# Row of s2 spread by two transfers through DRAM, reciprocals spread by SBUF transfers, no negated means, new places of the steps

## What is computed

```python
# layer 0: additive attention           x: (32, 256, 128), adj: (32, 256, 256) int
Wh = h @ W.T;  s1 = Wh @ a1;  s2 = Wh @ a2
e = leaky_relu(s1[:, :, None] + s2[:, None, :], 0.2);  e = where(adj == 0, -inf, e)
x = layernorm(x + softmax(e) @ Wh)
# layer 1: bilinear attention logits, softmax, two products, ELU
x = layernorm(x + elu(x @ W_1 + (att @ x) @ W_2))
# layer 2: attention with 4 heads of 32, output projection, ReLU
out = concat_heads(softmax(mask(q @ k.T * scale)) @ v)
x = layernorm(x + relu(out @ Wo + bo))
# layer 3: relational convolution; with relation 1 alone it is
v = (h + b) * sigmoid(g + bg);  x = layernorm(x + relu((adj == 1).T @ v))
```

## Time and profile before

| what | value |
|---|---|
| median of three runs | 498.07 us (496.0 to 498.63) |
| the profiled execution | 496.9 us, span of its instructions 495.0 us |
| PE, ACT, DVE, POOL busy | 95%, 86%, 83%, 75% |
| mean granted TensorE clock | 0.988 of full speed |
| mean DMA rate | 54 GB/s |

### The profile page before, as it was taken

The page is one execution under the profiler, slowest core; times in us unless marked ns, Lnnn a source line. Parts: engine busy times, 40 slices in busy tenths (PEclk is TensorE's granted clock), DMA queues, the critical chain, the costliest instruction groups (busy, mean ns, idle before and its releaser), DMA issues. The chain is left out here.

```text
span 495.0 us, 13988 instructions
## 1 busy us (share of the span) xinstructions
PE 468.4 (95%) x3872; PEld 402.3 (81%) x3872; DVE 410.8 (83%) x1605; ACT 428.0 (86%) x1261; POOL 370.6 (75%) x736
## 2 busy tenths in 40 slices
PE   6968999999999999999999999999999999999793
PEld 5756778988888888988888888888888888877572
DVE  5657898998888998898888988898898989876653
ACT  3558999999999999999999999999999999988750
POOL 1365576788888888888888888888888888986523
PEclk9989999999999999999999999999999999999997
DMA  7211111122112221222112221221123100000011
GB/s 219 74 44 44 44 54 52 40 63 66 40 48 66 66 66 54 54 66 63 36 56 66 65 60 51 66 65 43 45 66 87 34 23 13 23 24 23 22 45 44
DMA packets 40222, 26.93 MB, mean 54 GB/s; under 512 B 2641, under 2 KB 39889, under 8 KB 40146
## 3 DMA queue, kind: packets, MB, share of 16 engines
q1 hardware_dynamic: 40146, 26.03, 18.4%
HBM read 17.63 MB, written 8.39 MB: 53 GB/s over the span
## 5 line engine op out<-in xcount | busy, mean ns | idle before, releaser
L1211 POOL TENSOR_SCALAR x<-y,minus_mean,rstd 128x128 f32<-128x128 f32 x244 | 144.8, 601 | 6.8 <-issue 5.1
L788 ACT ACTIVATE p<-p,nmax 128x256 f32<-128x256 f32 x256 | 128.5, 530 | 0.4 <-DVE nmax L981 0.4
L981 DVE CUSTOM_DVE_ANT_0 p<-ps,neg 128x256 f32<-128x256 f32 x256 | 90.7, 420 | 2.3 <-PE ps L564 2.3
L1193 POOL TENSOR_TENSOR rstd<-ve,minus_half 128x2 f32<-128x2 f32 x128 | 91.1, 712 | 0.0
L575 PE MATMUL ps<-ident,p 128*128 128x128 f32 x512 | 78.0, 275 | 4.1 <-DVE nmax L981 3.4
L1186 POOL TENSOR_SCALAR ve<-stats 128x2 f32<-128x2 f32 x128 | 24.6, 192 | 72.3 <-DVE stats L896 64.9
L797 ACT COPY p2T<-ps 128x512 f32<-128x512 f32 x128 | 75.2, 590 | 1.3 <-PE ps L575 0.5
L575 PEld LDWEIGHTS ps<-ident,p 128*128 128x128 f32 x512 | 61.3, 143 | 9.3 <-DVE nmax L981 4.0
L788 ACT ACTIVATION_READ_ACCUMULATOR p<-p,nmax 128x1 f32 x256 | 56.1, 219 | 0.0
L896 DVE BATCH_NORM_STATS2 stats<-y 128x6 f32<-128x256 f32 x128 | 54.1, 423 | 1.5
L1175 POOL TENSOR_TENSOR relu<-relu,neg 128x512 f32<-128x512 f32 x32 | 37.1, 1161 | 21.1 <-ACT relu L757 21.1
(11 more groups left out here) (130 smaller groups left out, 1210.3 us busy)
## 6 DMA issues: line engine op xcount, KB each, us to landing
adj_in<-in_adj_dram SPq DMA_DIRECT2D x32, 256.0 KB, 3.0
xT<-in_xT_dram SPq DMA_DIRECT2D x32, 128.0 KB, 2.1
x_in<-in_x_dram SPq DMA_DIRECT2D x32, 128.0 KB, 2.1
x_aside<-x SPq DMA_DIRECT2D x32, 128.0 KB, 2.1
out_dram<-x SPq DMA_DIRECT2D x32, 128.0 KB, 2.9
l_w<-in_l_w_dram SPq DMA_DIRECT2D x1, 257.0 KB
l_w<-in_l_w_dram SPq DMA_DIRECT2D x1, 256.0 KB
first_w<-in_first_w_dram SPq DMA_DIRECT2D x1, 129.0 KB, 2.2
```

Of the source, the lines that this page charges most:

```text
L788: last = nc.scalar.activation(p2(n)[:, k, a, :], p2(n)[:, k, a, :], ACT.Exp, bias=nmax2(n)[:, k, a:a + 1], scale=-1.0, accum_out=sum2(n)[: ...
L981: last = nc.vector.tensor_tensor_reduce(p2(n)[:, k, a, :], bank("sc2", n, a)[:, k * N:(k + 1) * N], neg2(n)[:, k, :], -1.0, HIGHEST, ALU.a ...
L1193: nc.gpsimd.tensor_tensor(rstd[layer](n), ve[layer](n), minus_half[:, :], ALU.pow)\
L1211: last = nc.gpsimd.tensor_scalar(dst[:, k, 0:D], y_t[layer](n)[:, k, :], minus_mean[layer](n)[:, k:k + 1], rstd[layer](n)[:, k:k + 1], ALU ...
```

## The change

The row of s2 no longer goes through PE, but for the first three graphs (`PE_ROWS = 3`). `proj0` has a further column, 0.2 s2, beside s2. `s2_out` (SP) writes these two columns, in pieces of 8 bytes, to a DRAM tensor of 256 by 2 values per graph; `s2_in` waits for that transfer and reads the 2 KB back to each of the 128 partitions; `e0` takes s2 and 0.2 s2 from there, both in SBUF with a stride of two. `s2_rows` and `c_s2` stay for graphs 0 to 2 alone.

The reciprocals are transposed as they are, 128 by 8, in one transpose; `c_rs` copies 8 partitions of 128 columns to `rs_turned`, and `rs_in` (SP) spreads them with two transfers within SBUF, each from 4 partitions to 128, each row read 32 times. `rs_rep` is gone.

`var` no longer computes minus the mean; `norm` and `end_norm` subtract the mean. `xw0` has four buffers for three, `s2row` three for two. `PLAN` has new places for all steps.

```diff
-    "sync": [("ld_xT", 6707), ("ld_adj", 7906), ("ld_w", 8043), ("ld_x", 8602), ("aside", 16291), ("store", 19013)],
+    "sync": [("ld_xT", 6202), ("ld_adj", 7343), ("ld_w", 7608), ("s2_out", 7830), ("s2_in", 8655), ("ld_x", 9440),
+        ("rs_in", 15141), ("aside", 18952), ("store", 19263)],
...
+PE_ROWS = 3
...
+    **{step: (0, PE_ROWS) for step in ("s2_rows", "c_s2")},
+    **{step: (PE_ROWS, 0) for step in ("s2_out", "s2_in")},
...
+            def rs_in(n):
+                sp.wait_ge(sem("rs_sb"), n + 1)
+                free(sp, "rs_row", n, "onT_sb")
+                for k in range(T):
+                    sp.dma_start(rs_row(n)[:, k * P:(k + 1) * P],
+                                 rs_turned(n)[k * HEADS:(k + 1) * HEADS].rearrange("h (a i) -> h a i", a=1)
+                                 .broadcast_to((HEADS, DK, P))).then_inc(sem(f"rs_in{n % RING['rs_row']}"), 16)
+
+            def s2_out(n):
+                sp.wait_ge(sem("wh_sb"), n + 1)
+                sp.dma_start(s2_dram[n].rearrange("(t p) c -> p t c", p=P), xw0(n)[:, :, 1:3])\
+                    .then_inc(sem(f"s2_out{n % 2}"), 16)
+
+            def s2_in(n):
+                sp.wait_ge(sem(f"s2_out{n % 2}"), 16 * ((n - PE_ROWS) // 2) + 16)
+                free(sp, "s2row", n, "e0_ready")
+                sp.dma_start(s2row(n).rearrange("p j c -> p (j c)"),
+                             s2_dram[n].rearrange("(a j) c -> a (j c)", a=1).broadcast_to((P, 2 * N)))\
+                    .then_inc(sem(f"s2_in{n % RING['s2row']}"), 16)
...
-                pe.wait_ge(sem("rs_rep_ready"), n + 1)
-                for k in range(T):
-                    last = pe.transpose(o[:, k * P:(k + 1) * P], rs_rep(n)[:, k, :], ident[:, :])
-                last.then_inc(sem("rs_ps"), 1)
+                pe.wait_ge(sem("rsum2_ready"), n + 1)
+                pe.transpose(o[0:T * HEADS, 0:P], rsum2(n).rearrange("p t h -> p (t h)"), ident[:, :])\
+                    .then_inc(sem("rs_ps"), 1)
...
-                nc.scalar.copy(rs_row(n), bank("rs_rows", n)[:, 0:N]).then_inc(sem("rs_sb"), 1)
+                rows = slice(0, T * HEADS)
+                nc.scalar.copy(rs_turned(n)[rows, :], bank("rs_rows", n)[rows, 0:P]).then_inc(sem("rs_sb"), 1)
...
+                if n < PE_ROWS:
+                    dve.wait_ge(sem("s2_sb"), n + 1)
+                    row = bank("s2_rows", n)[:, 0:N]
+                else:
+                    dve.wait_ge(sem(f"s2_in{n % RING['s2row']}"), 16 * ((n - PE_ROWS) // RING["s2row"]) + 16)
+                    row = s2row(n)[:, :, 0]
...
-                dve.wait_ge(sem("rs_sb"), n + 1)
+                dve.wait_ge(sem(f"rs_in{n % RING['rs_row']}"), 16 * T * (n // RING["rs_row"] + 1))
...
-                nc.gpsimd.tensor_scalar(minus_mean[layer](n), stats[layer](n)[:, :, 1], -1.0, None, ALU.mult)\
-                    .then_inc(sem(f"mean{layer}_ready"), 1)
...
-                                                   minus_mean[layer](n)[:, k:k + 1], rstd[layer](n)[:, k:k + 1],
-                                                   ALU.add, ALU.mult)
+                                                   stats[layer](n)[:, k, 1:2], rstd[layer](n)[:, k:k + 1],
+                                                   ALU.subtract, ALU.mult)
```

More of the change, by code:

```diff
@@ L26 @@
 PLAN = {
-    "sync": [("ld_xT", 6707), ("ld_adj", 7906), ("ld_w", 8043), ("ld_x", 8602), ("aside", 16291), ("store", 19013)],
[6 rows of a table removed]
-        ("c_prep_c", 11302), ("c_prep_d", 11955), ("c_xT1", 12119), ("c_prep_b", 12238), ("c_tT", 12318),
[11 rows of a table removed]
+    "sync": [("ld_xT", 6202), ("ld_adj", 7343), ("ld_w", 7608), ("s2_out", 7830), ("s2_in", 8655), ("ld_x", 9440),
+        ("rs_in", 15141), ("aside", 18952), ("store", 19263)],
+    "tensor": [("proj0", 7737), ("s2_rows", 9639), ("prep_a", 10904), ("pT0", 11038), ("agg0", 11310),
+        ("prep_c", 11344), ("flag", 11765), ("prep_b", 11841), ("prep_d", 11905), ("xT1", 11960), ("tT", 12149),
[4 rows of a table added]
+        ("c_prep_c", 11630), ("c_xT1", 12058), ("c_prep_d", 12070), ("c_tT", 12428), ("c_prep_b", 12476),
[11 rows of a table added]
 }
 RING = {
[1 row of a table removed]
[1 row of a table added]
     "x1": 3, "xT1": 2, "tT": 2, "xw1": 3, "relu": 2, "p1": 2, "p1T": 2, "h": 2, "hexp": 2,
@@ L191, in build @@
         eq1 = ring("eq1", [T, N])
[L192 removed]
+        xw0_all = sb("xw0", [P, RING["xw0"], T, D + 4])
         xw0 = lambda n: xw0_all[:, n % RING["xw0"]]
[L194 removed]
+        s2row = ring("s2row", [N, 2])
         p0 = ring("p0", [T, N])
@@ L229, in build @@
         ve = [ring(f"ve{k}", [T], of="small") for k in range(4)]
-        minus_mean = [ring(f"minus_mean{k}", [T], of="small") for k in range(4)]
         rstd = [ring(f"rstd{k}", [T], of="small") for k in range(4)]
@@ L239, in build @@
         rsum2 = ring("rsum2", [T, HEADS])
-        rs_rep = ring("rs_rep", [T, D], of="rs_row")
+        rs_turned = ring("rs_turned", [P], of="rs_row")
         ps = ctx.enter_context(nc.psum_tensor("ps", [P, 8, 512], F32))
@@ L254, in build @@
         x3_dram = nc.dram_tensor("x3_aside", (B, P, T * D), F32, kind="Internal").ap()
+        s2_dram = nc.dram_tensor("s2_rows", (B, N, 2), F32, kind="Internal").ap()
         x_v = t["x"].rearrange("b (t p) d -> b p t d", p=P)
@@ L355, in _ @@
             sp.dma_start(first_w[:, :], t["first_w"]).then_inc(sem("w0_loaded"), 16)
-            run("sync", {"ld_adj": ld_adj, "ld_xT": ld_xT, "ld_x": ld_x, "ld_w": ld_w, "aside": aside, "store": store})
+            run("sync", {"ld_adj": ld_adj, "ld_xT": ld_xT, "ld_x": ld_x, "ld_w": ld_w, "rs_in": rs_in, "s2_out": s2_out, "s2_in": s2_in, "aside": aside, "store": store})
             for s in range(RING["x4"]):
@@ L712, in c_proj0 @@
                 free(act, "xw0", n, "agg_ps0")
-                nc.scalar.copy(xw0(n)[:, :, 0:D + 2],
-                               bank("proj0", n)[:, 0:T * (D + 2)].rearrange("p (t d) -> p t d", t=T))\
+                nc.scalar.copy(xw0(n)[:, :, 0:D + 3],
+                               bank("proj0", n)[:, 0:T * (D + 3)].rearrange("p (t d) -> p t d", t=T))\
                     .then_inc(sem("wh_sb"), 1)
@@ L899, in e0 @@
             def e0(n):
-                dve.wait_ge(sem("s2_sb"), n + 1)
+                if n < PE_ROWS:
[4 more added lines that the diff above has]
+                    row = s2row(n)[:, :, 0]
                 free(dve, "p0", n, "pT_ps0")
                 for k in range(T):
-                    last = nc.vector.scalar_tensor_tensor(out=p0(n)[:, k, :], in0=bank("s2_rows", n)[:, 0:N],
-                                                              scalar=xw0(n)[:, k, 0:1], in1=s2row(n),
-                                                              op0=ALU.add, op1=ALU.max)
+                    last = nc.vector.scalar_tensor_tensor(out=p0(n)[:, k, :], in0=row, scalar=xw0(n)[:, k, 0:1],
+                                                          in1=s2row(n)[:, :, 1], op0=ALU.add, op1=ALU.max)
                 last.then_inc(sem("e0_ready"), 1)
```

46 lines of the change are left out of this document (20 added, 26 removed), and 34 rows, old and new, of tables (PLAN, RING).

## The result

The changed kernel takes **527.25 us** (median of 4 runs, 524.8 to 529.8), the kernel before took 497.03 us beside it (4 runs, 495.13 to 498.63). The ratio is 1.061, with a 95% interval from 1.0543 to 1.0677. I had forecast 489.0 us and a range of 483.5 to 495.0: the wrong direction, by 38 us.

What follows compares the result with a forecast made beforehand. It took PE's instruction stream to set the 14.0 us period: -9.0 us there, +0.5 at the start and -0.5 at the end gave -9.0, from a median of 498.07 to 489.0 us; range 483.5 to 495.0.

Steps and rivals of the forecast that it cites:

- PE is the bound; a graph without `s2_rows` and with one transpose takes 0.3 us less: PE's stream in the saturated middle: 5.8 us from `s2_rows` and 3.2 us from `rs_rows`, 0.32 of 14.0 us a graph.
- POOL loses 1.3 of 11.7 us; it is clear: POOL, each graph: `rs_rep` (395 ns) and four `minus_mean` (0.22 us each) go, so POOL would not bind.
- The store of `x_aside`: SP's queue: its issue, 0.55 us, counted among 0 to 1.5 us of issues ahead of the reciprocals' transfers.
- None runs out: Moved steps `wo2`, `xT1` and `agg3` were claimed to keep enough room behind the steps they need; no cost.
- Row of s2, "price nothing": Transfers `s2_out` and `s2_in`: 5 to 6 us in a row, hidden within a period, so no cost.
- `e0` at +0.1 us a graph: DVE's `e0` reading s2 from SBUF instead of PSUM: -0.07 to +0.23 us a graph, taken as +0.1.
- Reciprocals, 2.1 to 6.0 us, hidden: Two SBUF-to-SBUF transfers ahead of `onT2`: path of 3.3 to 8.7 us within 10.4 us of PE's stream, no cost.
- My slower case: Rival: reciprocal transfers late for `onT2` on DVE, costing 0.5 us in each of 29 graphs, 503.5 us; chance 0.08.
- End, net -0.5: Last graph's drain: longer reciprocal path 0 to +1 us, `minus_mean` gone from the path -0.7 us, net -0.5 us.
- Start, +0.5: Pipeline fill: `proj0(3)` and its load ahead of the first `exp0`, `prep_c` behind `agg0`; +0.5 us, between -0.5 and +2.

Runs made afterwards that it cites:

- the mended kernel: Changed kernel with negated means back, `x_aside` store at 17800, `norm2` at 16300 ahead of `rsq3`, last three graphs' reciprocals the old way: 492.75 us, ratio 0.9912.
- norm2 at 16060: Changed kernel with negated means back, `x_aside` store at 17800, last three graphs' reciprocals the old way, `norm2` moved ahead of `norm3`: 498.1 us, ratio 1.0011.

## Why the prediction was wrong

The sum took what PE's stream loses, 9.0 us, as nearly the whole price, and put at nothing what the change does on POOL, on SP behind `s2_out` and in the order between POOL and PE. There it failed: a graph took 14.84 us and not 13.7, since PE waited about 1.0 us in each for POOL's `norm2`. Step by step:

- **"PE is the bound; a graph without `s2_rows` and with one transpose takes 0.3 us less":** right. Wherever nothing waits the period is 13.71 to 13.74 us. The number of graphs was somewhat high: in the kernel before, PE is at 100.00% only from 80 to 440 us, 26 graphs and not 27 or 29, and 26 times the measured 0.29 us are 7.5 us for the 9.0.
- **"POOL loses 1.3 of 11.7 us; it is clear":** wrong, and the first step that failed. I took away what was deleted and gave no price to what was edited: `norm` with `ALU.subtract` for `ALU.add`. It costs 0.36 us more for each of eight instructions (0.31 by the means of the whole runs), 2.4 to 2.8 us a graph, about twice what POOL lost. The trace of before had no such row for POOL, so it should have had a bound, as `e0` had. But the total was not the point either: POOL had room for it (498.95 us in the old order, 2.9 us in the mended kernel).
- **The store of `x_aside`:** I counted its issue in front of the reciprocals and never asked who waits for it. Its new place is 2.5 periods behind `norm2`, half a period ahead of the `norm2` that needs the buffer, and behind `s2_out`, which waits for `c_proj0`. Half a period is 7 us; the wait, the issue and 4.2 us of landing (2.1 in the earlier trace rows) use it. This is the dearest single part: 12.5 us by itself.
- **"None runs out" (the other moves):** I checked `wo2`, `xT1` and `agg3`, all of them PE against DVE. The narrow place was POOL against PE, at `norm2` ahead of `xT3`. In the old order `var3` and `rsq3` stand ahead of `norm2` too, and `norm3` far behind it; in the new one `norm3` stands ahead as well. Moving `norm2` in front of `rsq3` is worth 5.1 us with the other causes gone, so it makes up for that and is not the undoing of a move. I did not compare POOL's order before and after.
- **Row of s2, "price nothing":** right for the time of the two transfers (3.1 and 3.8 us, 6.9 for my 5 to 6, and hidden); wrong in that a transfer added to SP's queue brings a wait, for which the store behind it pays. `e0` at +0.1 us a graph held in this order (506 ns in the mean); in the old order, beside `rmask1`, it was +1.0.
- **Reciprocals, 2.1 to 6.0 us, hidden:** they took 6.2 to 6.5 us, just above the upper bound. The estimate by the Trainium skill (page "DMA: Bandwidth & Descriptors", section "Why a DMA increments its semaphore by 16 and not by 1") was up to 6.0 for the two; on how many engines they ran no run here shows. Hidden in the middle: yes (two waits). My slower case, late transfers, is not what happened here: it was priced at 503.5, and in the old order it is 553.5, since `onT2` was 2.0 us late in each graph.
- **End, net -0.5:** mis-sized. The transfers cost it 3.7 us, and about 2 more stay in the mended kernel (84.0 for 82.0 us). In the drain nothing covers a transfer, and I had given the new path 0 to 1.
- **Start, +0.5:** `agg3` of graph 0 came 0.1 us sooner in the changed kernel, 1.9 later in the mended one; inside the bounds, and no more than single executions scatter. The first `pT0` stood at 12.90 us where I had 12.8.

Still open: why `x_aside` lands in 3.7 to 4.3 us in the new order and in 2.1 in the old. The reciprocals' transfers were taken away and it stayed at 4.3; with s2's transfers gone as well it was 2.6. That points to s2's transfers, but the old order with them has 2.2. And the reciprocals' transfers can slow it too: with them alone in the old order, issued right ahead of it, it lands in 4.7 us, and in 2.9 when they are issued sooner. What stands shortly ahead in SP's queue seems to matter; no run isolates it.

## What to carry to other kernels

Price what an edit changes, not only what it deletes: another operator on the same tiles can cost more than the instructions that it saves, and differs by engine. For each step that a new order moves, ask whose buffer it frees and when that buffer is next needed: a store behind a queue's new wait closed a ring here. A price on an engine that is not the bound can be nothing or many microseconds, by what stands behind it on the path to the engine that is; so compare the order of the third engine too, and put causes back one at a time into a kernel that has none, since taken away one at a time they hide each other.

## What the runs showed of the hardware

- POOL's tensor_scalar of 128 x 128 f32 with two operands per partition takes 437 ns at least with (add, mult) and 793 with (subtract, mult); on DVE both take 342.
- Two SBUF-to-SBUF transfers that spread 4 rows to 128 partitions (64 KB each) land 6.2 to 6.5 us after the second one's issue. The two issues behind them on SP take 2.4 and 2.2 us in the changed kernel; in the new order without them the same issues took 0.61 and 0.38, and without s2's transfers either 0.34 and 0.38.
- A DVE instruction took 1.47 us for 0.47 when its second input was moved from PSUM to SBUF and POOL's relu mask ran beside it (the kernel before with s2's row through DRAM). `eq1` on DVE took 1.16 us for 0.42 beside the same mask (norm2 at 16060).
